# Moving 16x16 blocks over partitions by 32x32 transposes instead of DMA, in a decoder layer on one core

## The reference

```python
qkv = silu(causal_conv4(x @ Wqkv)); q, k, v = split(qkv)
beta = sigmoid(x @ Wb); g = -exp(A_log) * softplus(x @ Wa + dt_bias)
q, k = l2norm(q), l2norm(k)
def step(M, t):                       # M: [heads, 128, 128]
    M = M * exp(g_t)
    M = M + outer(k_t, (v_t - k_t @ M) * beta_t)
    return M, q_t @ M
out = rms(scan(step)) * norm_w * silu(x @ Wz); x = x + out @ Wout
```

## Time and profile before

| | |
|---|---|
| median of 3 runs | 1969.6 us (1968.1 to 1971.41) |
| the profiled execution | 1970.14 us, span 1968.2 us |
| mean granted clock of TensorE | 0.978 |
| PE busy | 1854.2 us, 94% |
| DVE busy | 1137.7 us, 58% |
| ACT busy | 904.5 us, 46% |
| POOL busy | 741.7 us, 38% |
| DMA | 228916 packets, 138592 of them under 512 B; mean 51 GB/s |
| L583, three products of the projections | 1024 matmuls each, 395 to 419 ns mean |
| DMA issues of the blocks: L451, L460, L470, L474 | 64, 32, 32, 64; 2.0, 2.9, 2.6, 2.3 us to landing |

### The profile page before, as it was taken

One profiled execution on the slowest core, in us unless ns is written; L12 is line 12 of the kernel. 1 busy time (PEld: TensorE's weight loads), 2 busy tenths in 40 slices (PEclk: granted clock), 3 DMA queues, 4 the chain that ended last, 5 costly groups with the idle time before them and its releaser, 6 DMA issues.

```text
span 1968.2 us, 45306 instructions
## 1 busy us (share of the span) xinstructions
PE 1854.2 (94%) x16842; PEld 1507.3 (77%) x16842; DVE 1137.7 (58%) x2096; ACT 904.5 (46%) x2940; POOL 741.7 (38%) x1141
## 2 busy tenths in 40 slices
PE   5799999999999999999999999999987899999999
PEld 4688888887888888887888788878876566656574
DVE  6756666665667575666667475656654352525334
ACT  2556463645465555646465455646464221212121
POOL 1346463635454454635454454636352000000000
PEclk9999999989999999999999899999997899999999
DMA  3012120202021221212021211112032403031200
GB/s 120 11 48 57 31 61 18 60 23 54 23 55 33 50 57 26 56 27 60 23 55 33 48 46 37 52 26 60 23 111 97 142 22 113 26 97 43 75 10 22
DMA packets 228916, 99.81 MB, mean 51 GB/s; under 512 B 138592, under 2 KB 212960, under 8 KB 228000
## 3 DMA queue, kind: packets, MB, share of 16 engines
q1 hardware_dynamic: 228768, 97.55, 18.9%
HBM read 69.86 MB, written 27.66 MB: 50 GB/s over the span
## 4 chain that ended last, share of the span: by engine, by line
PE 65%; issue 20%; DVE 10%; POOL 3%; ACT 2%; DMA 1%; DVEq 0%; POOLq 0%; SPq 0%; ACTq 0%
PE bank L583 28%; PE bank L898 4%; DVE vT L1407 3%; PE bank L717 3%; PE bank L848 2%; PE bank L857 2%; POOL o_rstd L1861 2%; PE bank L809 2%; PE bank L798 2%; PE bank L842 2%; PE bank L668 2%; PE bank L864 1%; PE bank L961 1%; PE bank L979 1%; PE bank L695 1%
## 5 line engine op out<-in xcount | busy, mean ns | idle before, releaser
L583 PE MATMUL bank<-x_hi,w_hi 128*128 128x512 f32 x1024 | 429.4, 419 | 17.5 <-DVE vT L1407 17.1
L583 PE MATMUL bank<-x_hi,w_lo 128*128 128x512 f32 x1024 | 405.9, 396 | 0.0
L583 PE MATMUL bank<-x_lo,w_hi 128*128 128x512 f32 x1024 | 404.3, 395 | 0.6 <-issue 0.6
L583 PEld LDWEIGHTS bank<-x_hi,w_hi 128*128 128x128 f32 x1024 | 195.0, 190 | 59.8 <-issue 18.1
L583 PEld LDWEIGHTS bank<-x_hi,w_lo 128*128 128x128 f32 x1024 | 194.0, 189 | 42.4
L583 PEld LDWEIGHTS bank<-x_lo,w_hi 128*128 128x128 f32 x1024 | 195.4, 191 | 32.2 <-issue 1.0
L1407 DVE SCALAR_TENSOR_TENSOR qT<-bank,cw,qT 128x511 f32<-128x511 f32 (+2 forms) x192 | 142.1, 746 | 51.2 <-ACT qT L1060 46.7
L1892 POOL TENSOR_TENSOR rstd<-ve,mhalf 128x1 f32<-128x1 f32 x32 | 17.6, 550 | 387.7 <-DVE ve L1653 387.7
L1407 DVE SCALAR_TENSOR_TENSOR vT<-bank,cw,vT 128x511 f32<-128x511 f32 (+2 forms) x192 | 143.0, 745 | 8.2 <-ACT vT L1060 3.7
L1407 DVE SCALAR_TENSOR_TENSOR kT<-bank,cw,kT 128x511 f32<-128x511 f32 (+2 forms) x192 | 143.4, 747 | 5.0
L1861 POOL TENSOR_TENSOR o_rstd<-o_ms,minus_half 128x4 f32<-128x4 f32 x64 | 70.4, 1100 | 169.3 <-DVE o_ms L1572 169.3
(11 more groups left out here) (221 smaller groups left out, 4282.6 us busy)
## 6 DMA issues: line engine op xcount, KB each, us to landing
w_raw<-in_w_heads SPq DMA_DIRECT2D x64, 256.0 KB, 4.4
o_d<-og SPq DMA_DIRECT2D x64, 256.0 KB, 2.6
o_raw<-o_d SPq DMA_DIRECT2D x16, 1024.0 KB, 6.4
gam<-gam_d SPq DMA_DIRECT2D x16, 768.0 KB, 4.9
x_in<-in_x SPq DMA_DIRECT2D x16, 256.0 KB, 3.7
blkN_d<-nT SPq DMA_DIRECT2D x64, 64.0 KB, 2.0
t<-blkT_d SPq DMA_DIRECT2D x64, 64.0 KB, 2.3
wo_raw<-in_w_out SPq DMA_DIRECT2D x4, 1024.0 KB, 8.6
```

What stands on the lines that cost most here:

```text
L583: last = mm(bank[bk][:, :], w[:, kind % 2, d, :], xx[:, d, b * S:(b + 1) * S], start=(n == 0), stop=(n == 3 * ND - 1))
```

## The change

The DMAs and both DRAM buffers go. VectorE does the moving with its transposes of 32x32 squares. For each of the four diagonal 32-squares (`NPAIR`, the strips of 32 partitions) it transposes the square of every unit, taken in an order in which row s, half i and unit u = (b, c) become partition (i, u). One transpose leaves in partition (i, u) the rows of both 16-blocks; a multiply with a column of 0 and 1 (`in_half`, one entry for each partition) and a select by the other column keep those of half i. On the way back two multiplies spread `blkT` into two halves with zeros where the other half belongs, and four transposes write the 32-squares of `t32`, steps of one row of t32 (512 bytes) apart. `in_half` is made on VectorE at the start, from ten operations on [128, 1] that wait for GpSimd's masks. On GpSimd `scaled_k` moves behind the substitution, and blkN is read by columns, since it now lies the other way round. `blk_wide` and `blk_second` lie in `y1`, which is free at the time.

```diff
+            dve.wait_ge(masks_set, 1)
+            tt(in_half[:, 1:2], tri[:, BLK - 1:BLK], tri[:, BLK - 1:BLK], ALU.subtract).then_inc(in_half_done, 1)
+            for k in range(NPAIR):
+                for edge, op in ((PAIR - 1, ALU.add), (BLK - 1, ALU.subtract)):
+                    dve.wait_ge(in_half_done, 2 * k + 1 + (op == ALU.subtract))
+                    at_edge = tri[:, k * PAIR + edge:k * PAIR + edge + 1]
+                    tt(in_half[:, 1:2], in_half[:, 1:2], at_edge, op).then_inc(in_half_done, 1)
+            dve.wait_ge(in_half_done, 2 * NPAIR + 1)
+            ts(in_half[:, 0:1], in_half[:, 1:2], -1.0, 1.0, ALU.mult, ALU.add).then_inc(in_half_done, 1)
...
                 last_masked_gram()
+                def blocks_apart():
+                    dve.wait_ge(nT_done, 4 * h + 4)
+                    dve.wait_ge(z16_mm, h)
+                    for k in range(NPAIR):
+                        rows = slice(k * PAIR, (k + 1) * PAIR)
+                        nc.vector.transpose(blk_wide[rows, :, :].rearrange("p t (i u) -> p t i u", i=2),
+                                            nT[rows, :, :, rows].rearrange("s b c (i t) -> s t i (b c)", i=2)).then_inc(blk_step, 1)
+                    dve.wait_ge(blk_step, 5 * h + NPAIR)
+                    ts(blk_second[:, :, :], blk_wide[:, :, BLK:PAIR], in_half[:, 1:2], None, ALU.mult).then_inc(blk_step, 1)
+                    dve.wait_ge(blk_step, 5 * h + 5)
+                    stt(blkN[:, :, :], blk_wide[:, :, 0:BLK], in_half[:, 0:1], blk_second[:, :, :],
+                        ALU.mult, ALU.add).then_inc(blkN_done, 1)
+                blocks_apart()
                 keys_kept(NC - 1)
...
                 conv(h, Q_, 2)
+                def blocks_back():
+                    dve.wait_ge(sub_step, SUB * h + SUB)
+                    for i in range(2):
+                        ts(blk_wide[:, :, i * BLK:(i + 1) * BLK], blkT[:, :, :].rearrange("p t s -> p s t"),
+                           in_half[:, i:i + 1], None, ALU.mult).then_inc(blkT_step, 1)
+                    dve.wait_ge(blkT_step, 2 * h + 2)
+                    for k in range(NPAIR):
+                        rows = slice(k * PAIR, (k + 1) * PAIR)
+                        nc.vector.transpose(t32[rows, :, :, rows].rearrange("t b c (i s) -> t s i (b c)", i=2),
+                                            blk_wide[rows, :, :].rearrange("p s (i t) -> p s i t", i=2)).then_inc(t32_ready, 1)
+                blocks_back()
                 if more:
                     split(h + 1, K_)
                 conv(h, Q_, 3)
...
                 tt(k_norm[:, :, :], k_sqe[:, :, :], half[:, :].rearrange("p (b c) -> p b c", b=B), ALU.pow).then_inc(knorm_done, 1)
-                for c in range(NC - 1):
-                    scaled_k(c)
                 pool.wait_ge(inv_set, 2 * h + 2)
-                pool.wait_ge(blkN_in, 32 * h + 32)
+                pool.wait_ge(blkN_done, h + 1)
...
-                    tt(products, blkN[:, j, j + 1:BLK].unsqueeze(2).to_broadcast([P, below, j + 1]),
+                    tt(products, blkN[:, j + 1:BLK, j].unsqueeze(2).to_broadcast([P, below, j + 1]),
...
+                for c in range(NC - 1):
+                    scaled_k(c)
                 pool.wait_ge(nT_done, 4 * h + 4)
```

More of the change, by code:

```diff
@@ L108, in layer @@
     consts_end = sb.end
+    in_half = sb("in_half", [P, 2])
     minus_half = sb("minus_half", [P, UNITS])
@@ L163, in layer @@
     blkN = at(place["y1"][0], "blkN", [P, BLK, BLK])
+    blk_wide = at(place["blkN"][1], "blk_wide", [P, BLK, PAIR])
+    blk_second = at(place["blk_wide"][1], "blk_second", [P, BLK, BLK])
+    assert place["blk_second"][1] <= place["y1"][1]
     blkT = at(place["w1"][0], "blkT", [P, BLK, BLK])
@@ L291, in layer @@
         sem(n) for n in ("qtr_done", "qsq_done", "qeps_done", "vtr_done", "nv_done", "qk_mm", "pT_done", "qg_done", "kg_done"))
[L293 to L294 removed]
+    in_half_done, blk_step, blkN_done, inv_set, sub_step, blkT_step, t32_ready, tT_done, t32_done = (
+        sem(n) for n in ("in_half_done", "blk_step", "blkN_done", "inv_set", "sub_step", "blkT_step", "t32_ready", "tT_done", "t32_done"))
     y16_mm, y16_done, z16_mm, z16_done = (sem(n) for n in ("y16_mm", "y16_done", "z16_mm", "z16_done"))
@@ L403, in _ @@
             load_weight(0, Z_)
-            sp.wait_ge(masks_set, 1)
-            sp.dma_start(blkT_d.rearrange("k u t s -> (k u) (t s)"),
-                         t32[0:NPAIR * UNITS, 0:2, :, :].rearrange("p b c s -> p (b c s)")).then_inc(blkT_zero, 16)
-            sp.wait_ge(blkT_zero, 16)
             def load_context(b):
@@ L445, in head @@
             def head(h, first, more):
-                sp.wait_ge(nT_done, 4 * h + 4)
-                hold(sp, "sp")
-                sp.wait_ge(z16_mm, h)
-                for k in range(NPAIR):
-                    sl = slice(k * PAIR, (k + 1) * PAIR)
-                    sp.dma_start(blkN_d[k].rearrange("u s t -> s u t"),
-                                 nT[sl, :, :, sl].rearrange("s b c t -> s (b c) t")).then_inc(blkN_out, 16)
                 if not first:
@@ L456, in head @@
                     store_gated(h - 1, NC - 1)
-                sp.wait_ge(blkN_out, 64 * h + 64)
-                for i in range(2):
-                    rows, sl = slice(i * P // 2, (i + 1) * P // 2), slice(i * BLK, (i + 1) * BLK)
-                    sp.dma_start(blkN[rows, :, :], blkN_d[:, :, sl, sl].rearrange("k u s t -> (k u) s t")).then_inc(blkN_in, 16)
                 load_gam(h)
@@ L466, in head @@
                     load_weight(h + 1, V_)
-                sp.wait_ge(sub_step, SUB * h + SUB)
-                for i in range(2):
-                    rows, sl = slice(i * P // 2, (i + 1) * P // 2), slice(i * BLK, (i + 1) * BLK)
-                    sp.dma_start(blkT_d[:, :, sl, sl].rearrange("k u t s -> (k u) t s"), blkT[rows, :, :]).then_inc(blkT_out, 16)
-                sp.wait_ge(blkT_out, 32 * h + 32)
-                for k in range(NPAIR):
-                    sl = slice(k * PAIR, (k + 1) * PAIR)
-                    sp.dma_start(t32[sl, :, :, sl].rearrange("t b c s -> t (b c) s"),
-                                 blkT_d[k].rearrange("u t s -> t u s")).then_inc(t32_in, 16)
                 if more:
@@ L1515, in head @@
                 conv(h, Q_, 2)
+                def blocks_back():
+                    dve.wait_ge(sub_step, SUB * h + SUB)
+                    hold(dve, "dve")
+                    for i in range(2):
+                        ts(blk_wide[:, :, i * BLK:(i + 1) * BLK], blkT[:, :, :].rearrange("p t s -> p s t"),
+                           in_half[:, i:i + 1], None, ALU.mult).then_inc(blkT_step, 1)
+                    dve.wait_ge(blkT_step, 2 * h + 2)
+                    hold(dve, "dve")
+                    for k in range(NPAIR):
[3 more added lines that the diff above has]
+                blocks_back()
                 if more:
@@ L1837, in head @@
                     tt(rows, rows, products, ALU.subtract).then_inc(sub_step, 1)
+                for c in range(NC - 1):
+                    scaled_k(c)
                 pool.wait_ge(nT_done, 4 * h + 4)
+                hold(pool, "pool")
+                pool.wait_ge(ke_done, 3 * h + 3)
                 hold(pool, "pool")
```

11 lines of the change are left out of this document (5 added, 6 removed).

## The result

The changed kernel takes **2113.5 us** (median of 4 runs, 2104.9 to 2115.7) against 1968.9 us of the kernel before on the same chip: a ratio of 1.072 (95% interval 1.070 to 1.075). The forecast was 2050 us with a range up to 2100. The direction and the two places were right, the size was not: 79 us were forecast and about 145 came.

A forecast was written before the change was run, and what follows sets the result against it. VectorE's unbroken stretch from the last nT to V's convolution was taken to set TensorE's pace. To 1970.1 us came 16 x (3.39 + 0.7) = 65.4, start 2.8, clock 11: 79, so 2050 us, range 2010 to 2100.

The forecast's parts named there:

- the price of the transposes with a step: VectorE's four strided transposes, each way: 3.15 us together, the middle of 2.49 (step free) and 3.81.
- Going apart: VectorE's added work between the last nT and V's convolution: net 3.39 us a head, all waited for by TensorE.
- Coming back: VectorE's multiplies and transposes after the substitution delay conv Q3; 0.7 us a head reach TensorE at the 16-blocks (L745).
- g_lo's pace: Step cost read from the g_lo row, 0.64 ns more an element: four transposes 3.81 us, going apart 4.05 net.
- GpSimd: k_norm starts 3.39 us later, but key scaling no longer stands ahead: substitution starts and ends about 0.4 us later.
- Clock: TensorE's clock falls behind the longer V wait in half of the heads: 11 us, bounds 0 and 34.
- Start: VectorE waits for masks and makes the mask column before the first statistics: 2.8 us later, bounds 2 and 3.5.
- DMA: Removing sixteen small transfers a head gains zero, because VectorE's wait for t32 wasn't the last.
- Rival 2: Step costs g_lo's pace or more, clock falls in most heads: 2083 us, 2110 with twice the step cost; chance 0.21.
- Rival 1: The step costs the transposes nothing, coming back is hidden, waits too short for the clock: 2017 us; chance 0.2.
- rival 3: Without the DMA round trip TensorE keeps its clock in the small matmuls, 44.5 us back: 1972 us; chance 0.04.
- rival 4: VectorE's 3.07 us a head wait at t32 reaches TensorE, at most 4 us: 2046; counted within the forecast's 0.55.

The follow-up runs named there:

- experiment 3: The changed kernel, with the four transposes of going apart reading with steps of 1, 2, 4 and 128 elements: 2094.8 us, ratio 1.067.
- experiment 1: The kernel before, all DMAs kept, with the going apart added as dead work and `in_half` made at the start: 2087.3 us, ratio 1.061.
- experiment 4: The changed kernel with 22 matmuls, whose products nobody reads, ahead of Z batch 0 in each head: 2103.5 us, ratio 1.070.
- experiment 8: The kernel before with half of the going apart as dead work (two of four transposes, selects on 64 partitions): 2046.7 us, ratio 1.040.

## Why the prediction was wrong, by its own steps

The step that failed is the price of the transposes with a step: 3.15 us for four was written, 4.47 and 4.56 were measured. It stands in both terms of the sum, going apart and coming back, and makes 2.7 of the 4.4 us a head by which they were short together (4.1 forecast, 8.5 by the measured values). The rest is w_lo (0.8), the dependent starts (0.5) and small things.

- **Going apart.** Forecast net 3.39 us a head, measured 5.14 from the waits. The transposes took 4.47 us instead of 3.15, the dependent starts 0.19 + 0.16 + 0.15 instead of 0.1 in all (an estimate for which I had no row), the multiply and the select 0.83 instead of 0.72; k_sqe fell to 0.165 us as forecast. 5.14 lies inside the bounds that the prediction gave (2.73 to 5.37), near their end: I took a middle between the fast end and g_lo's pace, and the true price was above g_lo's pace (3.81). The written reason, "a transpose has one source, of which each row shows a part", was no reason for a middle. Experiment 3 has the price, experiment 1 the effect.
- **GpSimd.** The substitution started 9.80 us behind the end of nT (793.63 - 783.83), where it was 7.60 (732.20 - 724.60, by the row of before below): 2.2 later, not 0.4. That is the same error of 1.8 us, carried on: k_norm stands behind k_sqe, which stands behind the going apart.

```profile
732.20 0.21 POOL L1833 TENSOR_TENSOR prod<-blkN,blkT 128x15 f32<-128x15 f32 x1
```

- **Coming back.** The two multiplies were right in size and reason (2.05 us with GpSimd at k_tok, forecast 2.3), the transposes not (4.56 for 3.15). I missed w_lo, 1.81 us for 1.01: kdT's products had moved beside it, here and in 9 of the other 14 heads that have a w_lo; in five it took 0.69. With the measured values the prediction's own sum gives: w_lo ends 29.28 us behind nT (813.11 - 783.83), before 19.72, so 9.56 later; less the 5.24 by which TensorE is late in this head, less the slack of 1.05, leaves 3.3 us, where 0.7 was forecast.
- **The sum, with these two terms mended,** is 5.24 + 3.3 = 8.5 us a head. From the end of nT to the 16-blocks the followed head took 35.52 us and 27.14 before, 8.4 more. From L722 in head 0 to L722 in the last head it is 1472.7 us (132.1 to 1604.8), and was 1351.7: 8.07 a head over 15 heads. L722 in head 0 stands 14.8 us later than L745 did, the start included, and from the last head's on it is 0.9 less: 134.9 of the 134.9 us by which the span grew. Without any term for the clock the two mended terms so give 16 x 8.5 + 2.8 = 139 us. The structure of the forecast held; the sizes of its two terms did not.
- **Clock.** Forecast: it falls in half of the heads and costs 11 us on top. It falls in all of them, and where the changed kernel's later wait stands behind it, it costs little beyond the chain (experiment 4); the 33.6 us in the first account are for the most part matmuls that fill what would have been a wait. Alone with the going apart it does cost, up to 37 us (experiment 1). The forecast let the clock's loss overlap with coming back's 0.7 us; that it would overlap with a larger coming back nearly whole, the prediction said in part, and only of rival 2.
- **Start.** Forecast 2.8, measured 2.6 at the first matmul. In the profiled execution a spell of the lower clock near 43 us added to it: where head 0's long wait ends TensorE is 5.5 us late (77.47, and 71.96).
- **DMA.** The forecast that removing it brings nothing fits what was seen: experiment 1 keeps all the DMAs and has the changed kernel's wait for V, and outside the stretch from nT to the 16-blocks a head of the changed kernel is 0.2 us shorter (62.7 for 63.0), at most 4 us in all. No run takes the DMAs away alone.
- **Rivals.** Rival 2 was what happened, and its second number, 2110 us "with twice the step cost", is close. In part that is luck: it took 5.13 us for four transposes where 4.47 were measured, put the dependent starts at 0.1 and left w_lo as it was. I gave it 0.21 as a whole and drew the range short of it. Rival 1 is excluded by experiment 3. Of rival 3's 44.5 us at most 4 can be there, by the 0.2 us a head just named, and of rival 4 nothing was seen.

In the changed kernel the clock's slower matmuls and the chain come out nearly equal. In ten heads w_lo takes 1.8 us, and in these TensorE waits at q. In the five with 0.69 TensorE's twelve matmuls behind the wait take 5.0 to 5.3 us instead of 4.2 to 5.1, and it comes to q 32.1 to 32.5 us behind nT, with no wait to speak of. In experiment 4, with the clock kept up, w_lo took 0.69 in two heads, and there TensorE came to q at 31.1; so in those five heads the lower clock costs about 1 us each. Why the short w_lo and the slower matmuls go together is not explained by any of these runs.

## What to carry to other kernels

When a 32x32 transpose on VectorE reads fp32 with a step of 16 bytes or more, or writes it with one of 512, count the full price, here 1.1 us for 512 elements instead of 0.7, and don't average between rows that disagree; write one small run or take the slow row. Before giving work to an engine, write down what stands behind it in its queue: the same instructions cost 145 us at one place and 34 at another. When a trace shows a lower clock behind a wait, follow the chain of the other engines past it first: the slow matmuls may lie in time that TensorE would have spent waiting.

## What the runs showed of the hardware

- The transposes' pace: 700 and 702 ns at steps of 4 and 8 bytes, 1083 to 1097 at 16 and 512 bytes read, 1114 when it is the write that has the step, for 32x512.
- VectorE's dependent starts, a wait on a semaphore of its own last instruction, leave 0.15 to 0.19 us idle.
- The multiplies back take 1.42 us for two beside the selects and 1.6 to 2.3 beside the key scaling in the heads of the changed kernel (alone they were not seen; the one at the going apart, which doesn't read crosswise, takes 0.35). w_lo, two SBUF inputs, goes from 0.69 to 1.81 us beside kdT.
- A wait of 3.6 us (experiment 8) was followed by the lower clock in 15 of 16 heads; one of 0.66 us, in the kernel before, in none.
